# Attention inside a transformer layer kernel: scores issued one head per quarter step, and the preparation of the next token pair moved to other steps

## The chip, the cores and the metric

The kernel runs on one NeuronCore of a Trainium2 chip. A time is the device time of one execution in microseconds (us); a kernel's time is the median of several executions. The core has five engines that run side by side and meet at semaphores: TensorE (PE, matmuls; PEld is its weight load), VectorE (DVE), ScalarE (ACT), GpSimd (POOL) and SyncE (SP), which here issues the DMAs. Each engine takes its own instructions in order, so a waiting instruction holds everything behind it.

## What is computed

The input x has 8 batches of 1024 tokens with 256 channels. The layer is a mixture-of-experts feed-forward block, causal attention with 16 heads of 16 channels, and the same feed-forward block again. The change touches the attention alone, so only that part stands here:

```python
x = x + 0.5 * ffn(layernorm(x))
q, k, v = heads(layernorm(x))            # three 256x256 products with a bias
q, k = rope(q), rope(k)
att = softmax(where(causal, q @ k.T / sqrt(16), -1e10))
x = x + (att @ v) @ Wp.T + bp
x = x + 0.5 * ffn(layernorm(x))
```

## The kernel before

`build` runs three stages one after another: the first router and feed-forward block, `attention_block`, and the second router and feed-forward block. In `attention_block` the work is split into 32 groups, each of four heads of one batch (`GROUPS` = 8 batches x 4). A group has 12 steps (`STEPS`, `NS`), each one block of 128 keys against one half of the queries. Steps 0 to 3 are the first half, with 512, 128, 256 and 384 query columns; steps 4 to 11 are the second half, with 512, 128, 256, 384, 512, 512, 512 and 512 columns. Every step is cut into four quarters (`SHARES`, counted by c).

Three streams run through the steps.

The first is the attention of group g. TensorE computes the scores of step t+1 while step t is worked on (`scores`, L1748), one matmul for each of the four heads and, on the diagonal, a second small one that adds the mask (L1760). There are three PSUM banks of scores (`BANKS`), so the score of one head waits for the exponential of the score three before it. ScalarE takes the exponentials (`exponentials`, L1644), and TensorE multiplies them with v (`times_v`, L1763) in the third quarter of the step. In the kernel before, the scores of heads 0 and 1 are issued in quarter 0 and those of heads 2 and 3 in quarter 1.

The second is the row maxima of group g+1 (`ring`, L1734 for TensorE, L1499 for VectorE): 48 score products spread over the 12 steps, in three PSUM banks of their own, each reduced by VectorE (L1523 with a mask, L1526 without). After the maxima of one half are complete, VectorE splits them into three bf16 parts in a few tiny instructions between ring items (`split_peaks`, L1538 to L1547). TensorE transposes the parts (the ring item FIRST in step 5, the item SECOND in the last quarter of step 11, L1739), VectorE copies them out (L1514), and SP stores them to HBM and loads them back into q (`move_peaks`, L1292 to L1300). The first scores of a half wait for that load (`peak_loaded`, L1753).

The third is the preparation of a pair of token tiles n = g + 6 (`LEAD` = 6; 32 pairs): layer norm, the products for q, k and v, rope, and a split into three bf16 parts that go to HBM. A group finishes pair n-1 (`finish`) and then begins pair n (`prepare`). All of it goes through one PSUM bank, `prep_ps`, so its links follow one another strictly:

- transpose_qk of tile 0 (PE) -> first_parts (ACT, L1626) -> leave (DVE, L1496) -> transpose_qk of tile 1 -> first_parts -> leave -> transpose_x of the new pair (PE, L1691) -> xt_high (ACT, L1621) -> xt_low (DVE, L1475) -> product_qk of tile 0 (PE, L1700, three parts) -> add_bias_qk (DVE, L1482) -> product_v of both tiles -> add_bias_v (DVE, L1488) -> product_qk of tile 1 -> add_bias_qk.
- beside it: leave -> second_parts (ACT, L1631) -> third_parts (POOL, L1391) -> the stores of the pair (SP, `store_pair`, L1264), and add_bias_qk -> rope (POOL, L1375 to L1387, three stages) -> transpose_qk in the next group.

The order on each engine is written out by hand in the five `body` functions, by step t and quarter c. SP's order in a group is: the first o store, `store_pair` (five DMAs, waits for third_parts), `load_group` for group g+2 (thirteen DMAs, L1277), then `move_peaks` of both halves of group g+1, then the second o store. All of SP's DMAs go through one queue.

Groups 0 to 25 both finish and prepare a pair, group 26 only finishes one, and groups 27 to 31 do neither.

## Time and profile before

| | us |
|---|---|
| median of three runs (lowest, highest) | 2821.29 (2819.83, 2828.41) |
| the profiled execution | 2818.96 |
| its span in the profile | 2817.2 |
| PE busy, share of the span | 80% |
| DVE, ACT, POOL busy, shares | 60%, 42%, 34% |
| mean granted TensorE clock | 0.911 |

The profile is one execution as the hardware recorded it. Its page says how long each engine was busy, and its views list groups of instructions, waits and who ended them, and all instructions in order of time. The attention's main loop, from the first exponential of group 0 to the last of group 31, runs from 757.85 to 2127.35 us of the span. Busy shares alone don't say what sets the time there; the waits and the order in one group do. Below, "into the group" counts from the start of the group's first exponential; group 9 starts at 1158.77 us.

### The profile page before, as it was taken

What the parts mean: (1) busy time and instruction counts of PE and PEld (TensorE: products, weight loads), DVE (VectorE), ACT (ScalarE), POOL (GpSimd) and SP (SyncE); (2) the same over time, 40 slices, a digit from 0 to 9 for tenths busy, and PEclk for the clock granted to TensorE, in tenths of its full rate; (3) what the DMA queues carried; (4) which work ended last, traced back from release to release, by engine and by line L of the source; (5) the groups of instructions that cost most, each with busy time, mean ns of one, the idle gap of its engine ahead of it and who ended that gap; (6) DMA issues with size and microseconds to landing.
All of it is one profiled execution on the core that took longest, in us unless ns stands there. A gap on an engine that the chain in (4) does not pass through costs nothing. (4 is left out here: it accounts for less than half of the span.)

```text
span 2817.2 us, 43211 instructions
## 1 busy us (share of the span) xinstructions
PE 2262.0 (80%) x14545; PEld 1447.2 (51%) x14545; DVE 1698.4 (60%) x5181; ACT 1188.5 (42%) x2442; POOL 959.5 (34%) x1280
## 2 busy tenths in 40 slices
PE   6569999925688988888898888887993654899997
PEld 6558888823233333333333333333331654788886
DVE  7335555432677776777767677776761764455553
ACT  1134444401155555555555555554662111344443
POOL 3724434236233332332323332331001465244432
PEclk9999999955699998999999999999996775899999
DMA  9453222023353544536354453534323522522320
GB/s 343 171 187 105 71 102 74 24 81 81 88 106 84 107 96 91 107 71 121 74 98 106 84 101 76 106 84 88 81 47 104 162 91 85 194 76 71 106 68 20
DMA packets 227564, 284.00 MB, mean 101 GB/s; under 512 B 21432, under 2 KB 171896, under 8 KB 225296
## 3 DMA queue, kind: packets, MB, share of 16 engines
q1 hardware_dynamic: 215056, 248.68, 35.9%
q0 software_dynamic: 12288, 32.58, 3.2%
q8 instruction: 115, 1.88, 0.3%
q14 instruction: 105, 0.86, 0.1%
HBM read 154.78 MB, written 127.66 MB: 100 GB/s over the span
## 5 line engine op out<-in xcount | busy, mean ns | idle before, releaser
L1644 ACT ACTIVATE at_probs<-at_score_ps 128x512 f32<-128x512 f32 (+3 forms) x1536 | 648.8, 494 | 522.6 <-PE at_score_ps L1760 380.9
L1523 DVE CUSTOM_DVE_ANT_0 at_junk<-at_max_ps,at_causal 128x128 f32<-128x128 f32 (+3 forms) x1024 | 491.0, 486 | 215.0 <-PE at_max_ps L1745 207.8
L1757 PE MATMUL at_score_ps<-at_q,at_k 99*128 99x512 bf16 (+3 forms) x1536 | 449.3, 338 | 90.6 <-ACT at_probs L1644 48.9
L1745 PE MATMUL at_max_ps<-at_k,at_q 96*128 96x512 bf16 (+3 forms) x1536 | 455.7, 341 | 10.2 <-DVE at_peak L1526 5.9
L1526 DVE TENSOR_REDUCE at_peak<-at_max_ps 128x1 f32<-128x512 f32 x512 | 352.2, 688 | 151.3 <-PE at_max_ps L1745 148.9
L1037 DVE TENSOR_TENSOR f_hid_lo<-f_hid,f_hid_hi 128x512 fp32r<-128x512 f32 x256 | 177.5, 693 | 322.1 <-ACT f_hid_hi L1061 321.6
L1770 PE MATMUL at_o_ps<-at_probs,at_v 128*32 128x512 f32 (+3 forms) x3072 | 342.7, 519 | 0.1
L1099 PE MATMUL f_y_ps<-f_w_hi,f_hid_hi 128*128 128x256 f32 x1024 | 292.9, 286 | 49.7 <-DVE f_xe L1015 28.9
L1058 ACT ACTIVATE f_hid<-f_hid_ps 128x512 f32<-128x512 f32 x256 | 153.3, 599 | 415.3 <-PE f_hid_ps L1084 415.0
L1745 PEld LDWEIGHTS at_max_ps<-at_k,at_q 96*128 96x128 bf16 x1536 | 130.0, 99 | 351.7 <-DVE at_peak L1523 146.7
L1099 PE MATMUL f_y_ps<-f_w_hi,f_hid_lo 128*128 128x256 f32 x1024 | 291.4, 285 | 0.0
L1099 PE MATMUL f_y_ps<-f_w_lo,f_hid_hi 128*128 128x256 f32 x1024 | 290.3, 283 | 0.0
L1757 PEld LDWEIGHTS at_score_ps<-at_q,at_k 99*128 99x128 bf16 x1536 | 144.2, 100 | 262.2 <-ACT at_probs L1644 151.5
L1375 POOL TENSOR_TENSOR at_by_cos<-at_qk,at_cos 128x512 f32<-128x512 f32 x64 | 81.6, 1274 | 533.5 <-DVE at_qk L1482 533.5
L960 POOL TENSOR_SCALAR f_xn<-f_xe 128x256 f32<-128x256 f32 x120 | 164.1, 1374 | 217.5 <-PE f_xt_ps L1072 167.7
L1099 PEld LDWEIGHTS f_y_ps<-f_w_hi,f_hid_hi 128*128 128x128 f32 x1024 | 194.6, 190 | 72.8 <-issue 41.2
L1760 PE MATMUL at_score_ps<-at_hide_bf,ident_bf 128*128 128x128 bf16 x1024 | 220.0, 227 | 0.0
L1099 PEld LDWEIGHTS f_y_ps<-f_w_lo,f_hid_hi 128*128 128x128 f32 x1024 | 194.2, 190 | 9.1
L1099 PEld LDWEIGHTS f_y_ps<-f_w_hi,f_hid_lo 128*128 128x128 f32 x1024 | 194.2, 190 | 0.0
L1391 POOL TENSOR_TENSOR at_part<-at_rest,at_part 128x512 bf16<-128x512 f32 x64 | 73.9, 1155 | 307.3 <-ACT at_part L1631 307.3
L1084 PE MATMUL f_hid_ps<-f_xt_hi,f_w_hi 128*128 128x512 f32 x512 | 167.7, 409 | 2.8 <-DVE f_xt_lo L1006 2.8
L1061 ACT CAST f_hid_hi<-f_hid 128x512 fp32r<-128x512 f32 x256 | 158.8, 620 | 8.2
(174 smaller groups left out, 3693.4 us busy)
## 6 DMA issues: line engine op xcount, KB each, us to landing
f_w_raw<-in_w SPq DMA_DIRECT2D x32, 1024.0 KB, 7.7
qk<-at_part SPq DMA_DIRECT2D x96, 256.0 KB, 2.9
at_q<-qk SPq DMA_DIRECT2D x192, 128.0 KB, 4.9
at_k<-qk SPq DMA_DIRECT2D x192, 128.0 KB, 7.7
expert_in<-r_zeros SPq DMA_DIRECT2D x16, 1040.0 KB, 11.3
f_xe<-expert_in SPq DMA_DIRECT2D x32, 520.0 KB, 7.3
v_rows<-at_v_out SPq DMA_DIRECT2D x64, 256.0 KB, 3.7
at_v<-v_rows SPq DMA_DIRECT2D x32, 512.0 KB, 10.1
```

Of the source, the lines that this page charges most:

```text
L960: last = nc.gpsimd.tensor_scalar(xn[:, t, :], x[:, t, 0:C], x[:, t, MEAN:MEAN + 1], x[:, t, RSTD:RSTD + 1], ALU.subtract, ALU.mult)
L1037: v.tensor_tensor(hid_lo[f % NHID][:], hid[f % NHID][:], hid_hi[f % NHID][:].bitcast(F32), ALU.subtract).then_inc(hid_lo_ready, 1)
L1061: nc.scalar.copy(hid_hi[f % NHID][:], hid[f % NHID][:]).then_inc(hid_hi_ready, 1)
L1084: last = nc.tensor.matmul(hid_ps[f % 2][:], w[ws][:, cc, f * P:(f + 1) * P], x[b % 2][:, cc, :], start=(i == 0), stop=(i == 3 * CC - 1))
L1099: last = nc.tensor.matmul(y_ps[t][:], a[m][:, rows], w[ws][:, f, :], start=(f == 0 and i == 0), stop=(f == FC - 1 and i == 2))
L1523: v.tensor_tensor_reduce(junk[bank(k, r)][:, 0:w], src, causal[:, HALF - w:HALF], 1.0, LEAST, ALU.add, ALU.max, out).then_inc(max_used, 1)
L1526: v.tensor_reduce(out, src, AX.X, ALU.max).then_inc(max_used, 1)
L1644: a.activation(probs[t % 2][:, h, c0:c0 + w], score_ps[(GH * t + h) % BANKS][:, 0:w], ACT.Exp, scale=float(SCALE)).then_inc(exp_done, 1)
L1745: te.matmul(max_ps[bank(u, r)][:, 0:w], q[u][0:ROWS, h, i * P:(i + 1) * P], kk[u][0:ROWS, h, k0:k0 + w], start=True, stop=True).then_inc(m ...
L1757: last = te.matmul(out[:, 0:w], kk[u][:, h, j * P:(j + 1) * P], q[u][:, h, hf * HALF + c0:hf * HALF + c0 + w], start=True, stop=not diagonal)
L1760: last = te.matmul(out[:, 0:P], sh.ident_bf[:], hide_bf[:], start=False, stop=True)
L1770: last = te.matmul(o_ps[h * VW:(h + 1) * VW, c0:c0 + w], vv[u][:, j, h, :], probs[t % 2][:, h, c0:c0 + w], start=(t == FIRST_STEP[hf]), st ...
```

## The change

Work is the same before and after: no instruction is added and none removed. What changes is the order.

- TensorE issues one head's score in each quarter of a step, ahead of the other work of the quarter, where before it issued two in each of the first two quarters, behind the preparation's piece.
- The preparation is moved. In steps and quarters (t, c): transpose_qk of tile 1 from (3, 0), (3, 1) to (2, 1), (2, 2); transpose_x from (5, 0) to (3, 2); product_qk of tile 0 from (6, 1) to (6, 3) to (4, 1) to (4, 3); product_v from (8, 0), (8, 1) to (5, 2), (6, 1); product_qk of tile 1 from (10, 0) to (10, 2) to (8, 0), (9, 0), (10, 0).
- On VectorE: leave from (2, 0) and (4, 1) to (1, 3) and (3, 1); xt_low from (5, 3) to (4, 0); add_bias_qk of tile 0 from (7, 1) to (5, 1); add_bias_v from (8, 3) to (6, 3); add_bias_qk of tile 1 from (11, 1) to (10, 2).
- On ScalarE: second_parts of tile 0 from step 3 to step 2; xt_high from step 5 to step 4; second_parts of tile 1 from step 5 to step 4, behind xt_high.
- On GpSimd: the three rope stages of tile 0 from steps 8 to 10 to steps 6 to 8.

```diff
--- before.py
+++ after.py
@@ -1425,8 +1425,8 @@
                     if prepare:
                         if 5 <= t <= 7 and n + 1 < PAIRS:
                             invert_std(n + 1, [t - 5])
-                        if 8 <= t <= 10:
-                            rope(n, 0, t - 8)
+                        if 6 <= t <= 8:
+                            rope(n, 0, t - 6)
                         if t == 11:
                             rope(n, 1, 0)
 
@@ -1590,9 +1590,9 @@
                                 if has_place(ahead, r):
                                     ring(ahead, (k + (2 if t == NS - 1 else 1)) % SLOTS, r)
                         if finish:
-                            if (t, c) == (2, 0):
+                            if (t, c) == (1, 3):
                                 leave(n - 1, 0)
-                            if (t, c) == (4, 1):
+                            if (t, c) == (3, 1):
                                 leave(n - 1, 1)
                         if prepare:
                             if (t, c) == (1, 2):
@@ -1600,13 +1600,13 @@
                             stage = SHARES * (t - 2) + c - 1
                             if 0 <= stage < 6 and n + 1 < PAIRS:
                                 measure(n + 1, [stage])
-                            if (t, c) == (5, 3):
+                            if (t, c) == (4, 0):
                                 xt_low(n)
-                            if (t, c) == (7, 1):
+                            if (t, c) == (5, 1):
                                 add_bias_qk(n, 0)
-                            if (t, c) == (8, 3):
+                            if (t, c) == (6, 3):
                                 add_bias_v(n)
-                            if (t, c) == (11, 1):
+                            if (t, c) == (10, 2):
                                 add_bias_qk(n, 1)
 
             groups(dve, body)
@@ -1666,13 +1666,14 @@
                     if finish:
                         if t == 1:
                             first_parts(n - 1, 0)
+                        if t == 2:
+                            second_parts(n - 1, 0)
                         if t == 3:
-                            second_parts(n - 1, 0)
                             first_parts(n - 1, 1)
-                        if t == 5:
-                            second_parts(n - 1, 1)
-                    if prepare and t == 5:
+                    if prepare and t == 4:
                         xt_high(n)
+                    if finish and t == 4:
+                        second_parts(n - 1, 1)
                 if more:
                     exponentials(g + 1, 0)
                 copy_o(g, 1)
@@ -1745,20 +1746,19 @@
                 te.matmul(max_ps[bank(u, r)][:, 0:w], q[u][0:ROWS, h, i * P:(i + 1) * P], kk[u][0:ROWS, h, k0:k0 + w],
                           start=True, stop=True).then_inc(max_ready, 1)
 
-            def scores(g, u, t, pr):
+            def scores(g, u, t, h):
 
                 c0, w, diagonal = columns(STEPS[t])
                 hf, j = STEPS[t]
-                if t in FIRST_STEP.values() and pr == 0:
+                if t in FIRST_STEP.values() and h == 0:
                     pe.wait_ge(peak_loaded[hf], 16 * (g + 1))
-                for h in range(2 * pr, 2 * pr + 2):
-                    pe.wait_ge(exp_done, GH * (NS * g + t) + h + 1)
-                    out = score_ps[(GH * t + h) % BANKS]
-                    last = te.matmul(out[:, 0:w], kk[u][:, h, j * P:(j + 1) * P],
-                                     q[u][:, h, hf * HALF + c0:hf * HALF + c0 + w], start=True, stop=not diagonal)
-                    if diagonal:
-                        last = te.matmul(out[:, 0:P], sh.ident_bf[:], hide_bf[:], start=False, stop=True)
-                    last.then_inc(score_ready, 1)
+                pe.wait_ge(exp_done, GH * (NS * g + t) + h + 1)
+                out = score_ps[(GH * t + h) % BANKS]
+                last = te.matmul(out[:, 0:w], kk[u][:, h, j * P:(j + 1) * P],
+                                 q[u][:, h, hf * HALF + c0:hf * HALF + c0 + w], start=True, stop=not diagonal)
+                if diagonal:
+                    last = te.matmul(out[:, 0:P], sh.ident_bf[:], hide_bf[:], start=False, stop=True)
+                last.then_inc(score_ready, 1)
 
             def times_v(g, u, t):
                 c0, w, _ = columns(STEPS[t])
@@ -1802,8 +1802,8 @@
             pe.wait_ge(qkv_loaded[1], 16 * LOADS)
             for r in RING_STEPS[NS - 1]:
                 ring(1, 1, r)
-            for pr in range(2):
-                scores(0, 0, 0, pr)
+            for h in range(GH):
+                scores(0, 0, 0, h)
 
             def body(g, k, more, prepare, finish):
                 n = g + LEAD
@@ -1823,29 +1823,29 @@
 
                         for s in range(2):
                             for half in range(2):
-                                if finish and (t, c) == (3 * s, half):
+                                if finish and (t, c) == (2 * s, s + half):
                                     transpose_qk(n - 1, s, half)
                         if not prepare:
                             return
-                        if (t, c) == (5, 0):
+                        if (t, c) == (3, 2):
                             pe.wait_ge(rest_ready, 2 * n)
                             transpose_x(n)
                         for i in range(3):
-                            if (t, c) == (6, i + 1):
+                            if (t, c) == (4, i + 1):
                                 product_qk(n, 0, i)
-                            if (t, c) == (10, i):
+                            if (t, c) == (8 + i, 0):
                                 product_qk(n, 1, i)
-                        for s in range(2):
-                            if (t, c) == (8, s):
-                                product_v(n, s)
+                        if (t, c) == (5, 2):
+                            product_v(n, 0)
+                        if (t, c) == (6, 1):
+                            product_v(n, 1)
 
                     for c in range(SHARES):
+                        if t + 1 < NS:
+                            scores(g, k, t + 1, c)
+                        elif more:
+                            scores(g + 1, slot_round(g, k, 1)[0], 0, c)
                         piece(c)
-                        if c < 2:
-                            if t + 1 < NS:
-                                scores(g, k, t + 1, c)
-                            elif more:
-                                scores(g + 1, slot_round(g, k, 1)[0], 0, c)
                         if c == 2:
                             times_v(g, k, t)
                         places(c)
```

## Rows read from the trace of the kernel before

**Rows 1.** stretches of the loop: us, busy time of each engine, PEclk, DMA share, GB/s

```profile
757.85:1920.35 1162.50, 1008.82 (x6794) 436.42 (x6795) 843.71 (x2779) 623.98 (x1430) 362.52 (x582) 0.96 0.48 95
1158.77:1202.02 43.25, 37.35 (x264) 16.24 (x263) 32.89 (x108) 23.97 (x56) 14.21 (x23) 1.00 0.48 94
1654.25:1698.03 43.78, 38.75 (x264) 16.85 (x263) 32.03 (x106) 24.01 (x55) 14.21 (x23) 0.96 0.49 92
2000.38:2034.15 33.77, 31.47 (x228) 11.41 (x227) 25.56 (x92) 21.10 (x51) 0.00 (x0) 1.00 0.41 80
```

**Rows 2.** PE's waits over groups 0 to 26: us in total, times, longest us

```profile
PE at_score_ps L1757 <- ACT at_probs L1644: 42.2, 107, 1.0
PE at_score_ps L1757 <- issue: 36.3, 19, 7.6
PE at_max_ps L1739 <- DVE at_peak_part L1547: 32.5, 27, 1.8
PE at_prep_ps L1700 <- DVE at_xt_lo L1475: 31.0, 26, 1.2
```

**Rows 3.** SP in group 9, in order of time: start us, us, what, [idle before]

```profile
1178.94 1.52 SPq L1270 DMA_DIRECT2D qk<-at_part  x3
...
1189.12 0.36 SPq L1296 DMA_DIRECT2D peaks<-at_peak_t  x1
1199.15 0.71 SPq L1299 DMA_DIRECT2D at_q<-peaks  x1
```

**Rows 4.** PE in group 9, in order of time

```profile
1162.84 0.22 PE L1739 MATMUL at_max_ps<-ident_bf,at_peak_part 128*48 128x128 bf16 x1 [1.42 <-DVE at_peak_part L1547]
...
1166.09 0.22 PE L1760 MATMUL at_score_ps<-at_hide_bf,ident_bf 128*128 128x128 bf16 x1
1166.51 0.28 PE L1757 MATMUL at_score_ps<-at_q,at_k 99*128 99x256 bf16 x1 [0.20 <-ACT at_probs L1644]
...
1170.72 0.38 PE L1757 MATMUL at_score_ps<-at_q,at_k 99*128 99x512 bf16 x1
1172.05 0.39 PE L1757 MATMUL at_score_ps<-at_q,at_k 99*128 99x512 bf16 x1 [0.96 <-ACT at_probs L1644]
...
1200.01 0.60 PE L1745 MATMUL at_max_ps<-at_k,at_q 96*128 96x512 bf16 x2
1201.49 0.38 PE L1757 MATMUL at_score_ps<-at_q,at_k 99*128 99x512 bf16 x1 [0.87 <-issue]
```

**Rows 5.** DVE in group 9, in order of time

```profile
1161.74 0.96 DVE L1547 TENSOR_TENSOR at_peak_part<-at_peak_rest,at_peak_part 128x16 bf16<-128x16 f32 x1
...
1168.33 0.55 DVE L1523 CUSTOM_DVE_ANT_0 at_junk<-at_max_ps,at_causal 128x384 f32<-128x384 f32 x1
...
1168.81 0.69 DVE L1496 TENSOR_TENSOR at_rest<-at_prep_ps,at_part 128x512 f32<-128x512 f32 x1
...
1177.03 0.17 DVE L1547 TENSOR_TENSOR at_peak_part<-at_peak_rest,at_peak_part 128x16 bf16<-128x16 f32 x1
1177.11 0.69 DVE L1526 TENSOR_REDUCE at_peak<-at_max_ps 128x1 f32<-128x512 f32 x1
...
1181.57 0.68 DVE L1475 TENSOR_TENSOR at_xt_lo<-at_prep_ps,at_xt_hi 128x512 fp32r<-128x512 f32 x1
```

**Rows 6.** ACT in group 9, in order of time

```profile
1171.40 2.07 ACT L1644 ACTIVATE at_probs<-at_score_ps 128x512 f32<-128x512 f32 x4
1173.51 0.59 ACT L1636 COPY at_o_out<-at_o_ps 128x512 f32<-128x512 f32 x1
```

**Rows 7.** POOL in group 9, in order of time

```profile
1161.40 1.26 POOL L1375 TENSOR_TENSOR at_by_cos<-at_qk,at_cos 128x512 f32<-128x512 f32 x1 [11.53 <-DVE at_qk L1482]
...
1164.35 1.27 POOL L1387 TENSOR_TENSOR at_rot<-at_by_cos,at_by_sin 128x512 f32<-128x512 f32 x1
```

**Rows 8.** PE at the end of group 20, in order of time

```profile
1697.06 0.60 PE L1745 MATMUL at_max_ps<-at_k,at_q 96*128 96x512 bf16 x2
```

**Rows 9.** PE's waits in groups 27 to 31: us in total, times, longest us

```profile
PE at_score_ps L1757 <- ACT at_probs L1644: 6.7, 28, 0.4
```

## Prediction, made before the changed kernel was run

> **What bounds the kernel now.** I began with the page: PE is busy 80% of the span, and the change touches only the attention loop. So I read the stretches [rows 1]. [...] The preparation costs some 10 us a group, and in group 9 PE idles 5.9.
>
> PE's waits tell where [rows 2]: 42.2 us for exponentials, 36.3 put down to "issue", 32.5 for the parts of the maxima (L1547), 31.0 for xt_low. The "issue" wait needs the order in time. In group 9 PE finished its last maximum of step 10 at about 1200.4 and started the next group's first score only at 1201.49, 0.87 idle [rows 4]. That score needs the peaks that SP loads back. SP began the pair's stores at 1178.94, issued the peaks' store at 1189.12, behind the pair's five stores and the thirteen loads of group g+2, and could issue the load back only at 1199.15, when that store had landed; 2.34 us later the score starts [rows 3, 4]. So the loop has two bounds close to each other: PE's own order, and a DMA chain of 22.55 us that starts when GpSimd ends third_parts of tile 1.
>
> **The change, part by part.** I count from Z, the start of the transpose SECOND (1162.84 in group 9), to R, where PE is through with step 10 (1200.45), and from there to the next Z. Before: Z to R 37.6, R to Z 5.65, sum 43.25.
>
> Scores one by one. Where the fourth score of a step waits for the first exponential of the same step, PE starts it 1166.51 - 1166.09 = 0.42 after the mask matmul in front of it, where unheld it is 0.06 [rows 4]. That is 0.36 in narrow steps, about 0.25 in wide ones, and once 1172.05 - 1170.72 = 1.33 less 0.22 of its own, 1.1, where ScalarE had first_parts in front. Over 12 steps some 3.3 us a group. One score per quarter removes nearly all of it: the fourth is issued behind times_v, about 1 us later. Bounds 2.5 to 3.5, I take 3.3.
>
> Preparation. No matmul is added; what is to be priced is how far each link stands from the next. Durations: exponential of 512 columns 2.07 / 4 = 0.5, ScalarE's copies 0.59 [rows 6]; a ring item 0.55 to 0.69 on VectorE, leave 0.69, xt_low 0.68 [rows 5]; a maximum of 512 columns 0.38 on PE till it can be read, followed by the next after 0.22 [rows 4]. VectorE takes a ring item some 0.17 after it lands, and each hand-over costs about 0.05. Four places in the new order:
> - transpose_qk of tile 1 at (2, 1), behind leave at (1, 3). PE has two scores in between: it is there 0.6 after issuing the ring item of (1, 3). VectorE needs 0.33 + 0.17 + 0.48 + 0.69 + 0.05 = 1.7, and 0.35 more since normalize stands in front. PE waits 1.4.
> - transpose_x at (3, 2), behind leave at (3, 1). PE is there after 0.44; VectorE needs 0.38 + 0.17 + 0.61 + 0.69 + 0.05 = 1.9 and 0.4 for the leftover of measure. PE waits 1.9.
> - product_qk at (4, 1), behind xt_low at (4, 0). From the last score of step 4, PE is there after 0.9. ScalarE has the exponential (0.48 till it starts, 0.5), copy_o and xt_high (0.5 + 0.59), VectorE 0.68, hand-overs 0.1: 2.85. PE waits 1.9.
> - product_v at (5, 2), behind add_bias_qk at (5, 1). Between the last product_qk and it PE has 1.2; VectorE has four ring items, the copy of the peaks and the add: 2.9. PE waits 1.7.
>
> Together 6.9, and 0.7 where ring items find all three banks taken behind these. Bounds of the 7.6: 4.5 (if VectorE is ahead of the ring each time) and 9. What goes besides the 3.3: the wait for xt_low (31.0 / 26 = 1.2 a group) [rows 2] and about 1.3 of small waits, among them ring items behind VectorE. Z to R: 37.6 - 5.8 + 7.6 = 39.4. These waits stand in a row on PE, and while PE waits the ring and the scores behind it stand too, so nothing covers them.
>
> R to Z. The chain from R: the wait for the peaks (1.04 in group 9) goes if PE itself comes later. What is left is 4.6 (1162.84 less the score's start, 0.53 ahead of 1158.77). Moving add_bias_qk of tile 1 ahead, to (10, 2), takes 0.69 off VectorE there, but puts it ahead of R, where VectorE is behind PE: no gain, 4.6 again. It also starts rope earlier: by_cos to rot took 1165.62 - 1161.40 = 4.22 [rows 7], and now lies over all of split_peaks. L1547 took 0.96 at 1161.74, while by_cos ran, and 0.17 at 1177.03 [rows 5]: 0.79 lost to it already. The other split instructions never met GpSimd's work here; bounds 0 and 1.0 more each way (if the meeting goes, 0.8 is gained). I take 4.6 + 0.3 = 4.9. PE waits for L1547 at L1739 and the whole group is queued behind.
>
> [...]
>
> The sum at the full clock: 39.4 + 4.9 = 44.3, against 43.25. The DMA chain does not bind earlier: by the same steps third_parts of tile 1 ends at Z + 15.95, before at Z + 15.87 (its store at 1178.94 is Z + 16.1) [rows 3, 4], so the chain allows a score at about Z + 38.7 to 40 and PE comes at 39.4. Moves that cost nothing: rope of tile 0, third_parts and the stores of v have steps to spare (GpSimd is busy 14.21 of 43.25 [rows 1]).
>
> The clock. Group 20 had one fall of the granted clock (0.96) [rows 1] and ended its last maxima 1.57 later into the group than group 9 (1697.06 - 1654.25 = 42.81 against 41.24) [rows 1, 4, 8], yet took only 0.53 more: the wait for the peaks absorbed it. After the change that wait is mostly gone, so falls count in full. The loop's mean clock is 0.96, about one fall a group; at 1.2 falls of 1.57 a group takes 44.3 + 1.9 = 46.2, against 44.71: +1.5. The new waits of 1.9 us may add falls; they may also split existing idle. Bounds -0.7 (no falls at all) and +3.
>
> Groups 27 to 31 have no preparation and gain what the scores wait: 6.7 us shown [rows 9], nearer 12 with the tails of the matmuls in front counted as above. I take 14 with the earlier SECOND (bounds 7 and 17); the DMA chain, shorter there without stores, would stop them at about 30.5 us. Group 26 is bound by the chain, -1.
>
> Sum: 26 x 1.5 - 14 - 1 = +24 us on the profiled execution of 2818.96, so 2843; the median lies 2.3 above the profiled one: 2845 us. About 0.3% (8.5 us) is what a measurement can tell from no change.
>
> **The rivals.**
> - *The forecast*: new waits at four places outweigh the scores' hold. 2845; its own range +0.6 to +2.9 a group, 2822 to 2881. For it: the distances between links shrink from whole steps to one or two quarters. 0.45.
> - *Collision and cold clock*: rope over split_peaks delays Z by 1 us more, and two falls a group follow the waits: +3 a group, 26 x 3 - 15 = +63, 2884. It decides if L1538 or L1542 show long times. 0.18.
> - *They cancel*: +0.4 a group, 26 x 0.4 - 15 = -5, 2816; the waits are 1.1 smaller than I count. 0.15.
> - *Faster*: the other side. VectorE, idle 24% of group 9, is ahead of the ring, so the four waits come to 4 us instead of 7.6. The two leaves lie in front of third_parts as well, so the DMA chain starts some 1.7 earlier and the group ends at 42.6, bounded by the chain: -2.1 a group, 26 x -2.1 - 15 = -70, 2752. It decides where the waits stay under 6. 0.22.
>
> That the change doesn't do what it says is possible only for the scores' hold: if ScalarE's backlog holds them anyway, 3 us a group more, inside the second case.
>
> **How the numbers follow.** Slower 0.45 + 0.18 less 0.01 = 0.62; within 0.3% 0.15; faster 0.23. The range of 8 in 10 leaves out half of the faster case and the end of the second: 2765 to 2895.
>
> **What would show it.** In the changed kernel's trace: PE's waits for L1496 at transpose_qk and L1691, for L1475 and for L1482 at L1700, each over 1 us in every group (right), or under 0.5 (the faster case); the wait of L1757 for L1644 nearly gone; the "issue" wait at L1757 rare; L1538, L1542 and L1547 at 0.17 or near 1; store of the pair at Z + 16; groups 27 to 30 at 30 to 31.5 us. What makes me wrong first: the size of VectorE's backlog at those four places.

## The result, and the profile after

| | before | after |
|---|---|---|
| median of the paired runs, us (lowest, highest) | 2820.56 (2818.95, 2828.41) | 2908.9 (2901.31, 2915.51) |
| the profiled execution, its span | 2818.96, 2817.2 | 2915.51, 2913.7 |
| mean granted TensorE clock | 0.911 | 0.891 |

The change makes the kernel slower: ratio 1.0306, interval 1.0279 to 1.0334. The sign was forecast (2845, chance of slower 0.62); the size was not, +88 us where +24 was counted, and above the end of the range (2895). Between the two spans, 96.5 us apart, groups 0 to 25 account for 1268.22 - 1162.49 = +105.7, groups 26 to 31 for -8.1; the rest of the program is within 1.2.

Stretches of after, in the columns of [rows 1]: groups 0 to 25, group 9, group 11, group 28.

```profile
756.56:2024.78 1268.22, 1043.03 (x6793) 457.54 (x6793) 889.72 (x2778) 649.44 (x1430) 363.70 (x582) 0.91 0.44 87
1193.88:1241.13 47.25, 38.42 (x262) 16.82 (x262) 34.70 (x110) 25.26 (x56) 14.28 (x23) 0.96 0.43 85
1289.23:1339.99 50.76, 42.26 (x262) 18.48 (x262) 34.11 (x109) 24.90 (x56) 14.21 (x23) 0.87 0.42 80
2102.67:2134.45 31.78, 30.41 (x226) 11.72 (x226) 25.23 (x93) 22.20 (x51) 0.00 (x0) 1.00 0.35 85
```

A preparing group takes 1268.22 / 26 = 48.78 us against 1162.50 / 26 = 44.71 [rows 1], and the column PEclk says that the clock has a share in it: 0.91 against 0.96. The clock records of every trace here hold two values only, 1.00 and 0.50 (in after the column PEclk reads 0.50 for 1163.42 to 1170.22 and 1.00 for 1170.26 to 1200.92), so that is (1 - 0.91) / 0.5 x 48.78 = about 8.8 us a group at the lower level, against 3.6 before (the clock records of the two traces, without the rounding, give 8.7 and 3.8). The groups differ with it: 47.25 us at 0.96, 50.76 at 0.87.

PE's waits over groups 0 to 25 (us in total, times, longest), to be held against [rows 2]:

```profile
PE at_prep_ps L1692 <- DVE at_rest L1496: 45.4, 26, 2.1
PE at_prep_ps L1701 <- DVE at_qk L1482: 38.4, 26, 1.5
PE at_prep_ps L1701 <- DVE at_xt_lo L1475: 35.7, 26, 1.7
PE at_prep_ps L1731 <- DVE at_rest L1496: 34.8, 26, 1.5
PE at_max_ps L1740 <- DVE at_peak_part L1547: 34.0, 25, 1.4
PE at_max_ps L1746 <- DVE at_peak L1523: 23.4, 50, 0.7
PE at_score_ps L1757 <- ACT at_probs L1644: 1.0, 1, 1.0
```

In after, L1692 is transpose_x, L1701 the products, L1731 transpose_qk, L1740 the transposes FIRST and SECOND, L1746 the ring's maxima. The scores' hold is gone (42.2 to 1.0), and in its place stand four waits of the preparation, one each in every group, and the one for L1547 at SECOND. In group 9, PE in order of time (Z is the first line):

```profile
1199.40 0.22 PE L1740 MATMUL at_max_ps<-ident_bf,at_peak_part 128*48 128x128 bf16 x1 [1.36 <-DVE at_peak_part L1547]
...
1206.71 0.41 PE L1731 MATMUL at_prep_ps<-ident,at_rot 128*128 128x128 f32 x2 [1.07 <-DVE at_rest L1496]
...
1211.50 0.66 PE L1692 MATMUL at_prep_ps<-ident,at_xn 128*128 128x128 f32 x4 [1.73 <-DVE at_rest L1496]
...
1215.64 0.74 PE L1701 MATMUL at_prep_ps<-at_w_hi,at_xt_hi 128*128 128x512 f32 x2 [1.71 <-DVE at_xt_lo L1475]
```

The group starts at 1193.88, so SECOND begins 5.52 us into it; before it was 4.07 [rows 4]. Why, is on VectorE and GpSimd. VectorE, the tiny instructions of the split in order of time:

```profile
1195.24 0.64 DVE L1538 TENSOR_TENSOR at_peak<-at_peak 128x16 f32<-128x16 f32 x1
...
1196.02 0.68 DVE L1540 TENSOR_SCALAR at_peak_part<-at_peak 128x16 bf16<-128x16 f32 x1
...
1196.81 0.67 DVE L1542 SCALAR_TENSOR_TENSOR at_peak_rest<-at_peak,at_peak_part 128x16 f32<-128x16 f32 x1
...
1197.62 1.21 DVE L1545 CAST at_peak_part<-at_peak_rest 128x16 bf16<-128x16 f32 x1
1198.74 0.41 DVE L1523 CUSTOM_DVE_ANT_0 at_junk<-at_max_ps,at_causal 128x256 f32<-128x256 f32 x1
...
1199.09 0.16 DVE L1547 TENSOR_TENSOR at_peak_part<-at_peak_rest,at_peak_part 128x16 bf16<-128x16 f32 x1
```

GpSimd at the same time:

```profile
1194.59 1.27 POOL L1375 TENSOR_TENSOR at_by_cos<-at_qk,at_cos 128x512 f32<-128x512 f32 x1 [13.84 <-DVE at_qk L1482]
1195.81 1.65 POOL L1380 TENSOR_TENSOR at_by_sin<-at_qk,at_sin 128x256 f32<-128x256 f32 x2
1197.54 1.26 POOL L1387 TENSOR_TENSOR at_rot<-at_by_cos,at_by_sin 128x512 f32<-128x512 f32 x1
```

Read the ends, not the durations. L1538 ends at 1195.88, by_cos at 1195.86; L1542 ends at 1197.48, by_sin at 1197.46; L1545 ends at 1198.83, rot at 1198.80. L1547, started after rot, takes 0.16. L1540 ends at 1196.70, the first of the two by_sin instructions, which the line above merges, at 1196.66. Each of these four 16-element instructions waits for the end of the rope instruction that GpSimd is in: 3.20 us for four of them, which take 0.17 each in the kernel with rope behind the split. It is so in the whole trace: of the split's 288 instructions (both halves, all groups) 131 take over 0.3 us in after, against 24 before, and every one of them ends 0.03 to 0.04 us behind the end of a GpSimd instruction. The ring items between them (L1523), which read PSUM, keep their 0.28 and 0.41.

### The profile page after: what moved, and what is told of

Read it like the earlier page. It is cut to its first block and busy times, and to the rows that moved or that the text cites. A ratio compares the mean times of both kernels' runs of the same rounds, so it can differ in the third digit from the quotient of the medians.

```text
span 2913.7 us, 43211 instructions
## 1 busy us (share of the span) xinstructions
PE 2288.7 (79%) x14545; PEld 1466.5 (50%) x14545; DVE 1746.7 (60%) x5181; ACT 1219.2 (42%) x2442; POOL 961.0 (33%) x1280
## 5 line engine op out<-in xcount | busy, mean ns | idle before, releaser
L1644 ACT ACTIVATE at_probs<-at_score_ps 128x512 f32<-128x512 f32 (+3 forms) x1536 | 696.7, 494 | 646.4 <-PE at_score_ps L1760 479.2
L1523 DVE CUSTOM_DVE_ANT_0 at_junk<-at_max_ps,at_causal 128x128 f32<-128x128 f32 (+3 forms) x1024 | 486.5, 484 | 251.5 <-PE at_max_ps L1746 249.8
L1746 PE MATMUL at_max_ps<-at_k,at_q 96*128 96x512 bf16 (+3 forms) x1536 | 511.3, 356 | 43.9 <-DVE at_peak L1523 26.5
L1757 PE MATMUL at_score_ps<-at_q,at_k 99*128 99x512 bf16 (+3 forms) x1536 | 507.7, 340 | 9.8 <-issue 7.0
L1526 DVE TENSOR_REDUCE at_peak<-at_max_ps 128x1 f32<-128x512 f32 x512 | 353.1, 690 | 169.8 <-PE at_max_ps L1746 160.5
L1746 PEld LDWEIGHTS at_max_ps<-at_k,at_q 96*128 96x128 bf16 x1536 | 147.8, 102 | 425.5 <-DVE at_peak L1523 193.6
L1770 PE MATMUL at_o_ps<-at_probs,at_v 128*32 128x512 f32 (+3 forms) x3072 | 348.6, 527 | 1.4 <-ACT at_probs L1644 0.7
L1099 PE MATMUL f_y_ps<-f_w_hi,f_hid_hi 128*128 128x256 f32 x1024 | 292.8, 286 | 49.7 <-DVE f_xe L1015 28.9
L1760 PE MATMUL at_score_ps<-at_hide_bf,ident_bf 128*128 128x128 bf16 x1024 | 233.6, 230 | 0.0
L1757 PEld LDWEIGHTS at_score_ps<-at_q,at_k 99*128 99x128 bf16 x1536 | 155.6, 102 | 124.5 <-ACT at_probs L1644 42.7
L1701 PE MATMUL at_prep_ps<-at_w_hi,at_xt_hi 128*128 128x512 f32 (+1 forms) x256 | 99.8, 478 | 103.5 <-DVE at_xt_lo L1475 44.1
```

The lines of the kernel that those rows point to most:

```text
L1099: last = nc.tensor.matmul(y_ps[t][:], a[m][:, rows], w[ws][:, f, :], start=(f == 0 and i == 0), stop=(f == FC - 1 and i == 2))
L1523: v.tensor_tensor_reduce(junk[bank(k, r)][:, 0:w], src, causal[:, HALF - w:HALF], 1.0, LEAST, ALU.add, ALU.max, out).then_inc(max_used, 1)
L1526: v.tensor_reduce(out, src, AX.X, ALU.max).then_inc(max_used, 1)
L1644: a.activation(probs[t % 2][:, h, c0:c0 + w], score_ps[(GH * t + h) % BANKS][:, 0:w], ACT.Exp, scale=float(SCALE)).then_inc(exp_done, 1)
L1746: te.matmul(max_ps[bank(u, r)][:, 0:w], q[u][0:ROWS, h, i * P:(i + 1) * P], kk[u][0:ROWS, h, k0:k0 + w], start=True, stop=True).then_inc(m ...
L1757: last = te.matmul(out[:, 0:w], kk[u][:, h, j * P:(j + 1) * P], q[u][:, h, hf * HALF + c0:hf * HALF + c0 + w], start=True, stop=not diagonal)
```

## The experiments

Times are medians, ratios stand against the kernel before on the same chip; the group (mean of groups 0 to 25) and its clock are from each one's profile.

| kernel | us | ratio (interval) | group, us | clock there |
|---|---|---|---|---|
| before | 2820.6 | 1 | 44.71 | 0.96 |
| after | 2908.9 | 1.031 (1.028, 1.033) | 48.78 | 0.91 |
| scores alone | 2763.7 | 0.979 (0.974, 0.983) | 42.85 | 0.96 |
| preparation alone | 3063.1 | 1.085 (1.080, 1.090) | 53.73 | 0.86 |
| after, rope behind the split | 2830.9 | 1.003 (1.001, 1.005) | 45.50 | 0.97 |
| the same, split delayed by 1.4 | 2915.1 | 1.032 (1.029, 1.035) | 48.44 | 0.92 |
| after, links ahead of the ring | 2814.4 | 0.997 (0.994, 0.999) | 44.47 | 0.97 |
| after, both | 2771.7 | 0.983 (0.981, 0.984) | 43.36 | 0.97 |
| after, five waits filled | 2873.1 | 1.019 (1.014, 1.024) | 46.92 | 1.00 |
| after, two waits filled | 2878.5 | 1.019 (1.014, 1.024) | 47.33 | 0.96 |
| scores alone, peaks ahead | 2742.0 | 0.973 (0.971, 0.974) | 41.72 | 0.97 |
| the same, rope behind the split | 2727.1 | 0.967 (0.965, 0.969) | 41.26 | 0.97 |
| the same, leave and second_parts earlier | 2754.7 | 0.979 (0.974, 0.983) | 42.16 | 0.98 |
| rope behind the split, pair's store between | 2665.8 | 0.946 (0.944, 0.948) | 39.18 | 1.00 |

**Each half alone.** The kernel before with the scores of after:

```diff
+                        if t + 1 < NS:
+                            scores(g, k, t + 1, c)
+                        elif more:
+                            scores(g + 1, slot_round(g, k, 1)[0], 0, c)
                         piece(c)
-                        if c < 2:
-                            ...
```

> The scores' part of the change alone: one head per quarter ahead of the quarter's other work, the preparation where it was before. If the loss comes from the distances between the links of the preparation (my theory), this is faster than before: the 3.3 us a group that the fourth score waited go, until the DMA chain binds. The chain starts about 1.5 us earlier, so a prepared group should take about 43.2, not 44.7, and an unprepared one 31.9, as in the changed kernel: 2821 - 26 x 1.5 - 10 = 2772 us (2755 to 2795). If the loss comes from the scores' order (rival: a score ahead of the piece holds PE in each quarter), this is at 2821 or above, up to the changed kernel's 2909.

2763.7. PE's waits in it, over groups 0 to 26:

```profile
PE at_score_ps L1756 <- issue: 76.7, 26, 8.6
```

The scores' half is a gain of 57 us, and would be more: the "issue" wait, PE waiting for the peaks that come back over SP's queue, has doubled from 36.3 [rows 2] to 76.7.

The mirror, after with the scores two and two behind the piece as before:

> The preparation's part of the change alone, the scores two and two as before. If the distances between the links are the cause, the waits of the changed kernel stand (1.1 to 1.7 us each at four places, SECOND 5.5 us into the group) and part of the scores' hold comes back on top: 2909 plus 0 to 2.5 us a group, 2910 to 2975 us, 2935 taken. If the scores' order was the cause, this falls to about 2821. If the two parts only hurt together (rival), both this and the scores alone are near 2821.

3063.1, 128 us over what was expected and far above its range. The four waits are much as in after (37.9, 35.8, 35.6 and 34.3 us, each in 23 groups, so 1.5 to 1.65 each), the clock falls to 0.86, which is 15 us a group at the lower level; the expectation had put nothing to that. So the moved preparation is the whole loss, 242 us by itself, and the halves don't add up: the scores' half gives 57 us on the kernel before and 154 on this one, and part of that is the clock, 0.86 here and 0.91 in after; how large a part, no run shows.

**Rope and split at the same time.** After, but GpSimd starts the rope of tile 1 only when the split is through:

```diff
                         if t == 11:
+                            wait_apart(pool, peak_ready, 2 * (g + 2), sh.passed)
                             rope(n, 1, 0)
```

> The changed kernel with one wait more: GpSimd begins rope of tile 1 only after the four split instructions of the maxima (after L1547 in step 11), so that the two don't overlap. If rope over the split is what moved SECOND from 4.07 us into the group before to 5.52 after, the split instructions fall from 0.65 to 1.21 us to 0.17 us, SECOND stands at 4.1 to 4.4, and a prepared group loses 1.2 us, more if the granted clock falls less often: 2909 - 26 x 1.3 = 2875 us (2850 to 2885). If the four waits of the preparation and the clock make up the whole loss (rival), VectorE is late there anyway by its ring items, and the time stays within 5 us of 2909.

2830.9: 78 of the 88 us are gone, where 34 were expected, and the time is below the expected range. Of its profile, the group 9 stretch, then PE's waits over groups 0 to 26, then an instruction of the split:

```profile
1169.55:1214.10 44.55, 36.65 (x262) 16.36 (x262) 32.10 (x110) 24.91 (x57) 14.27 (x23) 1.00 0.48 91
```

```profile
PE at_prep_ps L1693 <- DVE at_rest L1497: 45.4, 26, 2.1
PE at_prep_ps L1702 <- DVE at_xt_lo L1476: 43.6, 26, 1.7
PE at_prep_ps L1702 <- DVE at_qk L1483: 38.5, 26, 1.5
PE at_prep_ps L1732 <- DVE at_rest L1497: 36.6, 27, 1.5
...
PE at_max_ps L1741 <- DVE at_peak_part L1548: 10.1, 27, 0.7
```

```profile
1171.79 0.17 DVE L1546 CAST at_peak_part<-at_peak_rest 128x16 bf16<-128x16 f32 x1
```

The four waits of the preparation are still there (the one for xt_low is 0.3 us a group larger, the others as they were); only the one at SECOND fell, from 34.0 to 10.1, and SECOND stands 4.07 us into group 9 again. The group at the full clock is 44.55, and the time at the lower level 0.03 / 0.5 x 45.5 = 2.7 us instead of 8.8. So the meeting costs 3.3 us a group: 1.45 directly (SECOND at 5.52 against 4.07; also 46.0, worked out below, less 44.55), the rest by the clock.

Is it the lateness of SECOND, or something else in the rope's new place? The same kernel, with a reduction, whose result nobody uses, put in front of the split's last instruction:

```diff
+                if stage == 3 and half == 1:
+                    v.tensor_reduce(idle_out[:], w_hi[:].bitcast(F32).rearrange("p c o -> p (c o)")[:, 0:1280], AX.X, ALU.max)
```

> The kernel with rope behind the split (2831 us), and in it one VectorE instruction of about 1.4 us (a maximum over 1280 values, its result unused) ahead of L1547 in step 11. GpSimd is idle meanwhile, so this puts the lateness of SECOND back and leaves the overlap with rope out. If SECOND's lateness is the whole effect, through the queue behind it on PE and through more falls of the clock, SECOND stands at about 5.4 us and the time goes back to the changed kernel's: 2895 to 2920, 2905 taken. If the overlap cost in another way too (rival), only the 1.4 us come back: 2831 + 26 x 1.3 = 2865.

2915.1, clock 0.92: all of it is back. VectorE's added instruction in group 9, and PE's wait:

```profile
1202.42 1.48 DVE L1549 TENSOR_REDUCE at_idle_out<-at_w_hi 128x1 f32<-128x1280 f32 x1
```

```profile
PE at_max_ps L1744 <- DVE at_peak_part L1551: 45.4, 26, 1.8
```

1.4 us of lateness at SECOND, with no meeting of rope and split, does what the meeting did: 84 us, 2.9 a group by the profiles (48.44 - 45.50), where PE's wait grew by 1.4 ((45.4 - 10.1) / 26).

**The four links.** After, with VectorE's leaves at (1, 3) and (3, 1), xt_low at (4, 0) and add_bias_qk at (5, 1) ahead of the ring items of their quarter instead of behind them:

```diff
                         ahead = ring_group(g, t)
-                        if ahead is not None:
-                            for r in share(t, c):
-                                ...
                         if finish:
                             if (t, c) == (1, 3):
                                 leave(n - 1, 0)
                             ...
+                        if ahead is not None:
+                            for r in share(t, c):
+                                ...
```

> The changed kernel with VectorE's order turned round inside four quarters: leave of (1, 3) and (3, 1), xt_low of (4, 0) and add_bias_qk of (5, 1) come ahead of the ring items of their quarter, not behind. If the four waits of PE are a ring item's way through VectorE (0.17 to be taken, 0.48 to 0.61 to work) plus the link, they shrink by 0.5 to 0.9 each where ScalarE is not the one awaited: transpose_qk 1.07 to 0.3, transpose_x 1.7 to 1.0, product_v 1.5 to 0.5, xt_low about the same since it waits for ScalarE. 26 x -2 = -52: 2857 us (2835 to 2885). If the waits come through ScalarE (exponentials in front of its copies; rival), VectorE waits in front of the link instead, the maxima are held behind it, and the time is at 2909 or above.

2814.4, again below the expected range (95 us gained, 52 expected). PE's waits, over groups 0 to 26 and into group 27:

```profile
PE at_prep_ps L1702 <- DVE at_xt_lo L1475: 44.4, 26, 1.7
PE at_max_ps L1741 <- DVE at_peak_part L1547: 29.1, 27, 1.4
PE at_prep_ps L1693 <- DVE at_rest L1496: 28.8, 26, 1.4
PE at_prep_ps L1732 <- DVE at_rest L1496: 22.9, 26, 1.0
PE at_score_ps L1758 <- issue: 19.5, 17, 6.5
```

The wait for at_qk is down to 8.2, those for the leaves by a third; the one for xt_low grew from 35.7 to 44.4, since PE comes there sooner and ScalarE's part of the link is as it was. These five waits are 2.1 us a group less ((188.3 - 133.4) / 26), the "issue" wait 0.5 more (12.9 us of the 19.5 lie in groups 0 to 25), and the group 4.3 less, with 2.7 us at the lower clock instead of 8.8, though rope and split still meet and SECOND still stands at 5.06 in group 9. Both edits together:

> The changed kernel with both: rope behind the split of the maxima, and VectorE's links ahead of the ring items of their quarter. Apart they gave -78 and -95 us. If their effects are apart, a prepared group goes from 45.5 (rope behind) by some 2.2 us of smaller waits to 43.3, or to about 42.6 where the DMA chain stops it, and few falls of the clock are left: 2831 - 26 x 2.7 = 2760 us (2740 to 2785). If both gained by the same falls of the clock (rival), the second brings little: 2790 to 2810.

2771.7, 12 us over what was expected. The two don't add: 4.3 and 3.3 us a group alone, 5.4 together. Either alone already brings the clock back to 0.97, and both together leave it there, so that part can be gained only once.

**The clock by itself.** After, with idle matmuls into the bank that the next ring item overwrites, put in front of the waits, so that PE works while it would wait (4, 7, 7 and 6 at the four places, 5 at SECOND):

```diff
+            def fill(g, u, r, times):
+                pe.wait_ge(max_used, place(g, r) + 1)
+                for _ in range(times):
+                    te.matmul(max_ps[bank(u, r)][:]..., sh.ident_bf[:], sh.ones_bf[:]..., start=True, stop=True)
```

> The changed kernel, in which PE does idle work in its five long waits: matmuls of 512 columns (ones, result overwritten by the next ring item) ahead of the awaited instruction, 4 at transpose_qk, 7 at transpose_x, 7 at product_qk, 6 at product_v, 5 at SECOND, each set a little shorter than the wait at the full clock. It adds work and takes no wait away. If the falls of the granted clock are what makes a prepared group 48.8 us and not the 45.3 that the waits alone give, the half-clock time falls from 8.7 us a group to near 0, and the time to 2909 - 26 x 3.3 = 2823 us (2810 to 2850). If the falls cost nothing because PE waits anyway (rival), the time stays at 2909 or rises.

2873.1. Groups 0 to 25, and group 9:

```profile
759.34:1979.19 1219.85, 1122.72 (x7542) 490.79 (x7542) 893.23 (x2778) 649.10 (x1429) 363.55 (x582) 1.00 0.46 90
1179.11:1226.16 47.05, 43.26 (x291) 18.92 (x291) 34.68 (x110) 25.00 (x57) 14.21 (x23) 1.00 0.45 86
```

The falls are gone, 36 us with them, though PE does more work. The miss of 50 us has four parts. The fill at SECOND waited for a bank and came late: the transpose started 1.0 us later than in after (6.52 us into group 9), 27 us over groups 0 to 25, and the same fill makes each unprepared group 0.9 longer, 4 us. The falls had cost less than I had put in: 48.78 less 46.0 (47.05 - 1.0), about 2.8 us a group and not 3.3, which is 13 us. And the 48.78 comes from the profiled execution of after, 6.6 us above its median. Filling only the two waits at transpose_x and product_qk:

> The same with the idle matmuls at two places only, transpose_x and product_qk, where the trace of the changed kernel has most of its falls (20 of 33 begin near 18 us into the group). If each place has its own falls, about two thirds of the gain: 2850 us (2835 to 2870). If the falls only move to the next wait (rival), 2890 to 2910.

2878.5, clock 0.96: half of the lower-clock time is gone, and 1.45 us a group. That lies between the two theories, and the clock records of the traces show why. In after 35 falls begin in groups 0 to 25, 20 of them 16 to 20 us into the group and 8 of them 28 to 32 us into it. With the two places filled, the 20 are gone and the 8 have become 19: part of the falls went, and more begin at a later place.

**The chain of DMAs, and a better kernel.** Back to the scores' half alone, where the loop waits for SP's queue. The peaks of the first half are moved ahead of the pair's store and the load:

```diff
                 store_o(g, 0)
+                if more:
+                    move_peaks(g + 1, slot_round(g, k, 1)[0], 0)
                 if finish:
                     store_pair(g + LEAD - 1)
...
                 if more:
-                    move_peaks(g + 1, slot_round(g, k, 1)[0], 0)
                     move_peaks(g + 1, slot_round(g, k, 1)[0], 1)
```

> The scores' part alone (2764 us) with SP's order changed: the peaks of the next group's first half are stored and loaded ahead of the pair's stores and the loads of group g+2, not behind them. In the scores' part alone PE waited 76.7 us at the first score of a group, nearly 3 us in each prepared group, for that load. If the DMA chain is what bounds that kernel, 2.35 us of load and its issue drop out and some 1.4 us of the peaks' store come in: the wait falls to about 1.7 us, now for the loads of q, k and v, and the time to 2764 - 26 x 1.2 = 2733 (2715 to 2750). If PE's own order bounds it (rival), it stays at 2764.

2742.0, inside its range. Then the rope behind the split as well:

> The same as the scores' part with the peaks ahead, and rope of tile 1 behind the split as well. There L1547 takes 0.96 us because of rope, and PE waits about 0.5 us at SECOND. If that delay runs on through the group, it gives 0.5 to 0.8 us a group: 2733 - 26 x 0.6 = 2717 (2700 to 2735), the fastest of all. If the loads bound the group whatever happens ahead of third_parts (rival), it equals the kernel without it within 5 us.

2727.1, 10 over what was expected. PE's longest wait over the whole loop, and SP in group 9, which starts at 1124.28:

```profile
PE at_score_ps L1758 <- DMA at_v<-v_rows: 55.3, 25, 8.8
```

```profile
1142.53 0.33 SPq L1296 DMA_DIRECT2D peaks<-at_peak_t  x1
1145.25 0.71 SPq L1299 DMA_DIRECT2D at_q<-peaks  x1
1146.21 1.51 SPq L1270 DMA_DIRECT2D qk<-at_part  x3
...
1155.86 0.43 SPq L1289 DMA_DIRECT2D at_v<-v_rows  x1
```

The peaks are in time now, and PE waits for the load of group g+2, whose maxima begin in step 11: 40.7 of the 55.3 us lie in groups 0 to 25. I took this chain, as in the kernel before, to start with third_parts, and drew that forward:

```diff
-                            if (t, c) == (4, 1):
+                            if (t, c) == (3, 3):
                                 leave(n - 1, 1)
...
-                        if t == 5:
+                        if t == 4:
                             second_parts(n - 1, 1)
```

> The kernel of e9 (scores one head at a time, the peaks' move put on SP's queue ahead of the store and the load, the rope of the product behind the split's items), with two steps drawn forward: VectorE's leave of transpose (n-1, 1) from item (4, 1) to (3, 3), and ScalarE's second parts of the same head from step 5 to step 4. In e9 the TensorE waits 54.5 us in 24 waits for the DMA that brings the new values (at_v), about 2.1 us a group of 41.26. If the chain of DMAs sets the group there, starting it 2 to 3 us sooner takes that wait down to 0.3 us or less, the group falls to about 39.5 us and the time by 26 x 1.75 = 45 us to 2682 us (2670 to 2705). If instead something else on TensorE's side takes the wait's place as soon as it goes (the waits for xt_low and for the transposes before, which would stay or grow since ScalarE and VectorE hold more work in steps 3 and 4), the time stays at 2715 to 2730 us with the wait for at_v still gone.

2754.7, slower than without, and neither theory's numbers. PE's waits over the whole loop:

```profile
PE at_score_ps L1758 <- DMA at_v<-v_rows: 57.5, 27, 8.8
PE at_max_ps L1747 <- DVE at_peak L1528: 31.0, 30, 1.1
```

The wait for at_v did not shrink, and PE now waits 1.1 us a group more for the ring (L1528; 1.0 us in all without the edit). In group 9, which starts at 1137.39, VectorE, GpSimd and PE show where that comes from:

```profile
1153.64 1.12 DVE L1544 SCALAR_TENSOR_TENSOR at_peak_rest<-at_peak,at_peak_part 128x16 f32<-128x16 f32 x1
```

```profile
1153.57 1.16 POOL L1392 TENSOR_TENSOR at_part<-at_rest,at_part 128x512 bf16<-128x512 f32 x1 [2.25 <-ACT at_part L1633]
```

```profile
1155.41 0.23 PE L1747 MATMUL at_max_ps<-at_k,at_q 96*128 96x128 bf16 x1 [1.12 <-DVE at_peak L1528]
```

It is the meeting of after once more, at another place: third_parts (POOL L1392), drawn forward, now runs over the split of the first half, L1544 takes 1.12 instead of 0.17 and ends 0.03 behind it, and the ring item for which PE waits stands right behind L1544. In the kernel without the edit no instruction of the split is held: all 288 take 0.16 to 0.18. The leave in its new place lies in front as well, but L1544's 0.95 us is most of the 1.12.

The rows of SP above say why the at_v wait stays: the pair's store stands behind the load of the peaks, and that stands 2.72 us behind their store, for which SP waits. With the edit third_parts ends 17.3 us into group 9 instead of 18.7, and the pair's stores are still issued only at 22.8, where it was 21.9. The chain starts with FIRST, not with third_parts. So the last kernel puts the pair's five stores into SP's waiting time, between the peaks' store and their load:

```diff
                 sp.dma_start(dr["peaks"][half]..., peak_t[:]).then_inc(peak_stored, 16)
+                if between:
+                    between()
                 wait_apart(sp, peak_stored, 16 * (2 * g + half + 1), sh.passed)
```

> The kernel of e9 with one change on SP: the pair's five stores are issued between the peaks' store and the peaks' load, instead of behind both. In e9's group 9 the peaks' store of the first half was issued at 18.25 us into the group (PE transposes FIRST at 17.50), the load back 2.72 later, when the store had landed, and the pair's stores 3.68 later at 21.93, though third_parts had ended at 18.74; the thirteen loads behind them were through at 32.0 and the last one landed 10.8 later, at 42.4, where PE waited for it (54.5 us in 24 waits over the loop). The run before this one showed that an earlier third_parts does nothing for this chain, since its start did not go by third_parts. If the chain goes by FIRST and the time SP stands waiting for the peaks' store, the stores and loads come 3 us earlier, the waits for at_v fall under 10 us in all, and the group takes 41.26 - 1.9 = about 39.4 us: 2727 - 48 = 2679 us (2665 to 2700). If something else (the waits for xt_low and for VectorE's ring items, or a queue that only moves as fast as the transfers land) takes its place, the time stays within 12 us of 2727.

2665.8, ratio 0.946, 13 under what was expected: 151 us faster than the kernel before on the same chip, and 243 faster than after, which ran on another chip. SP in group 9 (start 1110.94), PE's wait for the load over the whole loop, and groups 0 to 25:

```profile
1128.44 0.33 SPq L1296 DMA_DIRECT2D peaks<-at_peak_t  x1
1129.16 2.14 SPq L1270 DMA_DIRECT2D qk<-at_part  x3
1131.35 1.65 SPq L1273 DMA_DIRECT2D v_rows<-at_v_out  x2
1133.11 0.75 SPq L1301 DMA_DIRECT2D at_q<-peaks  x1
...
1139.80 0.43 SPq L1289 DMA_DIRECT2D at_v<-v_rows  x1
```

```profile
PE at_score_ps L1759 <- DMA at_v<-v_rows: 12.7, 8, 5.1
```

```profile
757.61:1776.30 1018.69, 948.59 (x6793) 425.46 (x6793) 807.74 (x2778) 646.54 (x1430) 364.30 (x582) 1.00 0.51 108
```

The last load is issued 28.9 us into the group instead of 31.6, the wait for it falls from 55.3 to 12.7 (from 40.7 to 3.1 in groups 0 to 25), and with the long waits the falls of the clock go too (0.97 to 1.00). The preparation is where the kernel before had it.

## Why the prediction was right in sign and wrong in size

By its own steps, with what was measured:

- *Scores one by one, -3.3 a group.* Right, as far as it can be read. The wait for L1644 went from 42.2 to 1.0, which is 1.6 a group. The scores alone took 1.9 us off the group while the "issue" wait grew by 1.5, which makes 3.4.
- *The four waits, 1.4, 1.9, 1.9 and 1.7.* In group 9 they are 1.07, 1.73, 1.71 and, the last one, 1.48 by the total (38.4 in 26). The sum is 6.0 where I had 6.9, and each was there in every group. The prediction had named VectorE's backlog here as what would make it wrong first; it was not. 6.0 is also just the mark that the faster rival had set itself, yet its 42.6 us a group came nowhere near: the mark was badly chosen. The waits for ring banks came to (23.4 + 9.5) / 26 = 1.3 where I had 0.7 (9.5 are those for L1526). Z to R at the full clock: 39.95 (46.0 less the 6.05 below; in the kernel with rope behind the split, at clock 1.00, it is 44.55 less 4.60, the same) against a forecast of 39.4, 0.55 off.
- *R to Z, 4.9.* This is the step that failed. It is 6.05 (SECOND at 5.52 into the group, and 0.53), 1.15 more. The prediction had the row that shows it, L1547 at 0.96 beside by_cos [rows 5], knew that the rope would now lie over the whole split, put a bound of 1.0 to it and took 0.3. Even the ends stood there to be compared: L1547 at 1162.70, by_cos at 1162.66 [rows 5, 7]. Five of the split's instructions could meet four of the rope's; four of them did, for 2.5 us over their free time, less the 1.0 that VectorE otherwise spends waiting for the ring between them. The row was right, but each of the five should have been priced by it; the bound of 1.0 was itself 0.45 short.
- *The sum at the full clock, 44.3.* It is 46.0; with the meeting taken out it is 44.55. So all but 0.25 of the 1.7 is the meeting.
- *The clock, +1.9.* It is +2.8. The number of falls was about right, 35 in 26 groups where 1.2 a group were counted; their length was not. They last 6.5 us each on average, 8.7 a group, where before 20 falls lasted 4.9 each, 3.8 a group. With the four waits in place the experiments show them to hang on how late SECOND is: without the meeting they are 2.7 us a group, with an artificial delay they are back. But it isn't SECOND alone: 1.9 us less at the links, with SECOND still late, brought the clock to 0.97 as well. What in the row of waits decides it stays open: each of these edits changed PE's total of waits too, so no run tells the place of a wait from the sum of them.
- *The DMA chain does not bind.* Right: the "issue" wait is gone (once, 0.4). (The 22.55 us of the chain count from the store's issue, Z + 16.1, and not from the end of third_parts, 0.2 us earlier.) The pair's store came at Z + 17.4, not Z + 16, without consequence, as PE was later still.
- *Unprepared groups, -14.* Half right: 31.8 to 33.0 us where 30 to 31.5 were named, -8 in all with group 26. The scores' hold that the view of waits shows (6.7, [rows 9]) was nearly all there was; the tails that I added to it were not.

Put together: 39.95 + 6.05 + 2.8 = 48.8 against 46.2, which is 2.6 x 26 = 68 us, and 7 for groups 26 to 31; the profiled execution, from which this is taken, lies 6.6 above the median. That is the rival "collision and cold clock" (2884, chance 0.18), by its own sign: L1538 and L1542 at 0.64 and 0.67. It named the two causes and had both too small (+3 a group; +4.07 measured).

So the right sign is partly luck. The forecast's own case, four new waits that outweigh the scores' hold, without the meeting, is the kernel with rope behind the split: it measured +9 us (ratio 1.003), where +24 was forecast. The +88 took the waits and the meeting together; taking away the meeting, or a third of the four waits (1.9 of 5.9 us a group, with the links ahead of the ring), brought the time back to within 10 us of the kernel before.

## What to carry to other kernels

Before moving work of GpSimd, list which short VectorE instructions on SBUF will run beside it and who waits for them: here 16-element ones were held until the GpSimd instruction beside them ended, up to 1.21 us where 0.17 is their free time. In the experiments third_parts, drawn forward, did it again over the first half's split. Put links of a chain where their neighbours leave room, not as close as the order allows: here the preparation's old distances hid everything but one wait, and the gain lay in the scores and in SP's queue. And before drawing the start of a chain forward, read in time order what its first transfer actually stands behind; here the wait on the queue was not for the data but for the transfer in front.

## What was not expected of the hardware

- The clock multiplied a small delay: 1.4 us a group at one place cost 2.9 us a group, 84 us in all, as PE spent 8 us instead of 2.7 a group at the granted clock of 0.50.
- VectorE's instructions with one SBUF input were held like those with two: L1540 took 0.68 and L1545 1.21, against 0.17 free.
- Idle matmuls paid: 749 more of them (7542 against 6793) made groups 0 to 25 shorter by 48 us.
- A small transfer took longer behind others: in after, the peaks' store behind the pair's and the group's transfers was issued at 1227.71 and SP could go on at 1236.86, 9.2 us later; put ahead of them (1142.53 to 1145.25, in the kernel with peaks ahead and rope behind the split) it took 2.7.
